# Value projections of a head moved one step later, their turns between and behind the block-inverse products

## What is computed

```python
q = silu(conv4(LN(x) @ Wq))                    # 8 heads of 128
k, v = silu(conv4(LN(x) @ Wk)), silu(conv4(LN(x) @ Wv))   # two keys and two values per token
q, k = q / |q| / sqrt(128), k / |k|
beta, g = 2 * sigmoid(LN(x) @ Wb), -exp(A_log) * softplus(LN(x) @ Wa + dt_bias)
for t in range(256):                           # per head, state 128 x 128
    state *= exp(g[t])
    for j in range(2):
        state += outer(k[t, j], (v[t, j] - k[t, j] @ state) * beta[t, j])
    o[t] = q[t] @ state
x += (rms(o) * norm_w * silu(LN(x) @ Wg)) @ Wo
x += top-k-masked, symmetrised similarity of ctx (256 x 256 per sequence) mixed with LN(x)
x += shared expert + two routed experts of eight, on LN(x)
```

## Time and profile before

| | us |
|---|---|
| median of 3 runs | 935.14 (933.33 to 941.7) |
| the profiled execution | 941.6, span 939.8 |
| attention part of its span (steps 0 to 10) | about 634 |
| busy: PE / DVE / ACT / POOL | 841.2 / 519.8 / 422.1 / 344.9 |

### The profile page before, as it was taken

One profiled execution on the slowest core, in us unless ns is written; L12 is line 12 of the kernel. 1 busy time (PEld: TensorE's weight loads), 2 busy tenths in 40 slices (PEclk: granted clock), 3 DMA queues, 4 the chain that ended last, 5 costly groups with the idle time before them and its releaser, 6 DMA issues. The chain is left out here.

```text
span 939.8 us, 16187 instructions
## 1 busy us (share of the span) xinstructions
PE 841.2 (90%) x5500; PEld 610.6 (65%) x5501; DVE 519.8 (55%) x1259; ACT 422.1 (45%) x929; POOL 344.9 (37%) x654
## 2 busy tenths in 40 slices
PE   4767999899999999999999876975999999999992
PEld 3333486686786776866867765864667667676761
DVE  3664638778887897887888655466411111111113
ACT  2656757456655656656666234213222222222220
POOL 1127466357368456564673480003420000000015
PEclk9879969879989899799899777796999999999997
DMA  7504133123150141141201301009673100110104
GB/s 187 141 25 111 23 85 90 24 59 67 24 121 5 38 109 21 31 98 24 56 19 24 89 2 29 2 1 366 238 241 109 33 24 32 33 33 22 33 24 128
DMA packets 107362, 66.30 MB, mean 71 GB/s; under 512 B 64864, under 2 KB 98720, under 8 KB 107296
## 3 DMA queue, kind: packets, MB, share of 16 engines
q1 hardware_dynamic: 99904, 59.52, 24.0%
q0 software_dynamic: 1536, 4.20, 1.5%
q10 hardware_dynamic: 5856, 1.73, 0.8%
HBM read 50.84 MB, written 14.58 MB: 70 GB/s over the span
## 5 line engine op out<-in xcount | busy, mean ns | idle before, releaser
L1129 DVE SCALAR_TENSOR_TENSOR y<-bank,cwh,y 128x510 f32<-128x510 f32 (+2 forms) x240 | 177.1, 743 | 57.9 <-ACT y L883 53.7
L633 PE MATMUL bank<-xnT,wbuf 128*128 128x512 f32 x320 | 163.0, 635 | 7.3 <-DVE y L1129 7.3
L1668 PE MATMUL bank<-f_wgu,f_xgT 128*128 x368 | 118.8, 466 | 0.0
L1946 DVE TENSOR_TENSOR f_act<-f_sg,bank 128x352 f32<-128x352 f32 x62 | 32.2, 521 | 143.8 <-PE bank L1668 141.5
L1433 POOL TENSOR_TENSOR term<-inv,blk 128x126 f32<-128x126 f32 (+22 forms) x248 | 87.8, 354 | 57.9 <-DMA blk<-a_blocks 39.1
L1785 ACT ACTIVATE f_sg<-bank 128x352 f32<-128x352 f32 x62 | 28.7, 464 | 161.1 <-PE bank L1668 152.7
L633 PEld LDWEIGHTS bank<-xnT,wbuf 128*128 128x128 f32 x320 | 57.9, 199 | 66.4 <-issue 53.8
L2021 POOL DMA_INDIRECT f_back<-slots_y,f_slot x16 | 15.4, 963 | 231.5 <-DMA slots_y<-f_yb 224.9
L1436 POOL TENSOR_TENSOR inv<-inv,term 128x126 f32<-128x126 f32 (+22 forms) x248 | 91.5, 369 | 19.4
L1713 PE MATMUL bank<-f_wdn,f_actT 128*128 (+1 forms) x372 | 91.5, 388 | 1.0 <-ACT f_actT L1798 0.8
L1668 PEld LDWEIGHTS bank<-f_wgu,f_xgT 128*128 128x128 f32 x368 | 66.2, 190 | 36.8 <-issue 7.6
(11 more groups left out here) (209 smaller groups left out, 1537.4 us busy)
## 6 DMA issues: line engine op xcount, KB each, us to landing
f_wgu<-in_exp_gu SPq DMA_DIRECT2D x8, 1408.0 KB, 9.7
f_wdn<-in_exp_dn SPq DMA_DIRECT2D x8, 640.0 KB, 10.5
dr<-sums SPq DMA_DIRECT2D x16, 256.0 KB, 4.5
ex<-sums SPq DMA_DIRECT2D x16, 256.0 KB, 4.5
blk<-a_blocks SPq DMA_DIRECT2D x16, 256.0 KB, 4.0
slots_x<-oT SPq DMA_DIRECT2D x24, 128.0 KB, 1.9
f_xg<-slots_x SPq DMA_DIRECT2D x24, 128.0 KB, 2.0
slots_y<-f_yb SPq DMA_DIRECT2D x23, 128.0 KB, 1.7
```

The source lines that it names most:

```text
L633: last = mm(bankA[p % 2][:, :], wbuf[A.par][:, kt, wblk, :], xnT[:, kt, (p % 2) * 512:(p % 2 + 1) * 512], start=kt == 0, stop=kt == 1)
L1129: v.scalar_tensor_tensor(out=y[p % 2][:, :, k:], in0=src[:, :, 0:SEQ - k], scalar=cwh[A.par][:, cb, 3 - k:4 - k], in1=y[p % 2][:, :, k:], ...
L1668: last = mm(gu[c][:, 0:FFH], xt[:, k, :], wgu[:, e, k, at:at + FFH], start=k == 0, stop=k == 1)
L1946: v.tensor_tensor(av[:, par, half * FFH:(half + 1) * FFH], sg[:, half, :], gu[2 * half + 1][:, 0:FFH], ALU.mult).then_inc(f_act, 1)
```

## The change

**Projections.** `projection(slot, A, B)` gives slots 0 to 5 to the keys and queries of head s and slots 6 to 9 to the values of head s-1. Step 0 thus has six projections, step 8 has four (before: ten and none), steps 1 to 7 have ten. All counts on `proj_done`, `conv_step` and `silu_done` follow `nth`. The value weights have a semaphore and a wait of their own.

**Turns.** The four `vtok` items move from slots 1, 2, 3 and 5 to slot 11 (behind t32), "blocks of 64" (behind x32) and LAST (behind p64, and behind t64). The two gates go to slots 3 and 5.

**Ends.** In step 0 `scalar_values` comes a slot earlier and without its exponentials; these, `dm` and `ex` stand in slot 11 (step 1: slot 8). The sixth norm stands in slot 11. 20 of the 24 zeroing DMAs go to step 1. `gwT` is loaded behind step 1's scatter. In step 8 top-k is spread: 8, then 4 operations in slots 1 to 3, 2 of the next tile in slots 4 to 8, and 10 at the end; `sigmoids` go to slot 9. The tap copies (`taps`) stand at POOL's end. The waits inside POOL's `norm`, and the order `dx`, `kn`, `sh`, `qE`, are untouched.

```diff
+        3: {"B": [("gate", 0)]},
+        5: {"B": [("gate", 1)]},
...
+        11: {"B": [("t32", 0), ("t32", 1), ("vtok", 0)]},
+        BLOCKS_64: {"B": [("x32", 0), ("x32", 1), ("vtok", 1)]},
+        LAST: {"B": [("p64", 0), ("p64", 1), ("vtok", 2), ("t64", 0), ("t64", 1), ("vtok", 3)]}}
...
-SCALARS_AT = 3
-EXP_AT = {0: 7, 1: 2}
+SCALARS_AT = 2
+EXP_AT = {0: 11, 1: 8}
+
+def projection(slot, A, B):
+    X = A if slot < 6 else B
+    return (X, slot) if X else None
...
-            for i in range(5):
+            for i in range(3):
                 sp.dma_start(wbuf[h % 2][:, :, i, :], head_weights(i, h)).then_inc(w_in[h % 2], 16)
+        def value_weights(h):
+            if h >= 2:
+                sp.wait_ge(proj_done, nth(h - 2, 9))
...
-        for m in range(SLOT_TILES):
-            sp.dma_start(dram["slots_x"][m], zero).then_inc(slots_zeroed, 16)
+        zero_slots(0, 4)
...
-                if b == 0 and kind != "kend":
-                    pe.wait_ge(silu_done, 10 * h + {"pair": 6, "vtok": 10}[kind])
+                if b == 0 and kind == "pair":
+                    pe.wait_ge(silu_done, nth(h, 5))
+                if b % 2 == 0 and kind == "vtok":
+                    pe.wait_ge(silu_done, nth(h, 8 + b // 2))
...
-                if A and slot < 10:
-                    proj(A, slot)
+                if slot < 10 and projection(slot, A, B):
+                    proj(*projection(slot, A, B))
...
-                if not A and tiles and slot == 5:
-                    topk(tiles[0], 8, 2 * ROUNDS)
+                if not A and tiles and 1 <= slot <= 3:
+                    topk(tiles[0], 4 * slot + 4, 4 * slot + 8)
+                if not A and tiles and 4 <= slot <= 8:
+                    topk(tiles[1], 2 * slot - 8, 2 * slot - 6)
...
-            if A:
-                start(A)
             if A and A.h == 0:
+                taps(0)
+                taps(1)
```

More of the change, by code:

```diff
@@ L105 @@
 FILL = {FIRST: {"B": [("pair", n) for n in range(BC // 2)]},
[L106 to L110, removed]
+        1: {"E": [("out", 0)]},
+        3: {"B": [("gate", 0)]},
+        4: {"E": [("out", 1)]},
+        5: {"B": [("gate", 1)]},
         6: {"B": [("kend", 0)]},
@@ L121, with projection_table, nth @@
 B_BANKS = 3
-SCALARS_AT = 3
-EXP_AT = {0: 7, 1: 2}
+SCALARS_AT = 2
[3 more added lines that the diff above has]
+    return (X, slot) if X else None
+def projection_table():
+    out = []
+    run_heads(lambda A, B, C, E: out.extend(projection(slot, A, B) for slot in range(10)))
+    return {(x[0].h, x[1]): i for i, x in enumerate(x for x in out if x)}
+PROJECTION = projection_table()
+def nth(h, p):
+    return PROJECTION[h, p] + 1
 def items_at(place):
@@ L361, in attention @@
     w_in = [w_in0, w_in1]
+    wv_in = [sem(f"wv_in{i}") for i in range(2)]
     wo_in = [wo_in0, wo_in1]
@@ L443, in sync_program, with zero_slots @@
         sp.wait_ge(zero_done, 1)
-        for m in range(SLOT_TILES):
-            sp.dma_start(dram["slots_x"][m], zero).then_inc(slots_zeroed, 16)
-        for k in range(KT_H):
-            sp.dma_start(gwT[:, k, :], dram["gate_w"].rearrange("e (k p) -> k p e", p=P)[k], allow_slow_non_contiguous=True).then_inc(mix_in, 16)
+        def zero_slots(first, end):
+            for m in range(first, end):
+                sp.dma_start(dram["slots_x"][m], zero).then_inc(slots_zeroed, 16)
+        zero_slots(0, 4)
         blocks = a_blocks.rearrange("(p x) -> p x", x=NB * NB)
@@ L502, in step @@
                 loads(A.h + 1)
+            if A and A.h:
+                value_weights(A.h)
             if 2 <= s <= HEADS:
@@ L530, in step @@
                 difference_rows(A.h + 1)
+            if s == 1:
+                zero_slots(4, SLOT_TILES)
             if B:
@@ L535, in step @@
             if s == 1:
+                for k in range(KT_H):
+                    sp.dma_start(gwT[:, k, :], dram["gate_w"].rearrange("e (k p) -> k p e", p=P)[k], allow_slow_non_contiguous=True).then_inc(mix_in, 16)
                 tiles_out()
@@ L1041, in step @@
             if A and s not in EXP_AT:
+                exp_table()
                 decays(A)
@@ L1055, in step @@
                     scalar_values()
-                if slot == EXP_AT.get(s, -1):
-                    decays(A)
-                    pair_decays(A)
                 if s == 1 and slot < 11:
                     context_copies(act, slot, slot + 1)
-                if s == HEADS and slot == 7:
+                if 2 <= slot and projection(slot - 2, A, B):
+                    silu(*projection(slot - 2, A, B))
+                if s == HEADS and slot == 9:
                     sigmoids()
-                if A and 2 <= slot:
-                    silu(A, slot - 2)
                 if A and 5 <= slot <= 10:
                     square(A, slot - 5)
-                if A and slot < 10:
-                    evac(A, slot)
+                if slot < 10 and projection(slot, A, B):
+                    evac(*projection(slot, A, B))
+                if slot == EXP_AT.get(s, -1):
+                    exp_table()
+                    pair_decays(A)
+                    decays(A)
+                    if s == 0:
+                        scalar_decays()
             fill(BLOCKS_64)
@@ L1299, in step @@
                     gate_ends()
-                if A and 1 <= slot <= 10:
-                    conv(A, slot - 1, (1,))
+                todo = projection(slot - 1, A, B) if 1 <= slot <= 10 else None
+                if todo:
+                    conv(*todo, (1,))
                 if C:
                     scan(C, slot)
-                if A and 1 <= slot <= 10:
-                    conv(A, slot - 1, (2, 3))
+                if todo:
+                    conv(*todo, (2, 3))
                 fill(slot)
@@ L1328, in step @@
                     norm_sum(A, 1)
+            if not A and tiles:
+                topk(tiles[1], 10, 2 * ROUNDS)
             fill(LAST)
@@ L1340, in gpsimd_program, with taps @@
         pool.wait_ge(small_in, 160)
-        def start(A):
-            h = A.h
-            if not isinstance(h, int) or h >= 2:
-                if some(30 * (h - 1)):
-                    pool.wait_ge(conv_step, 30 * (h - 1))
-            g.tensor_copy(cwh[A.par][:, :, :].rearrange("p a k -> p (a k)"),
+        def taps(h):
+            if h >= 2:
+                pool.wait_ge(conv_step, 3 * nth(h - 2, 9))
+            g.tensor_copy(cwh[h % 2][:, :, :].rearrange("p a k -> p (a k)"),
                           cw[:, :, :, :].rearrange("p h a k -> p h (a k)")[:, h, :]).then_inc(cwh_done, 1)
```

76 lines of the change are left out of this document (42 added, 34 removed).

## The result

The changed kernel takes 979.6 us (978.32 to 982.69, 4 runs) against 936.29 us of the kernel before (933.33 to 941.7, 4 runs): 1.046 times as long, 95% interval 1.040 to 1.052. The forecast was 986, slower by over 1% with a chance of 0.85. The sum came out near; several of its terms did not.

What follows compares the result with a forecast made beforehand. The prediction took PE's own work and the loop through POOL's inversion as level bounds. Terms -18 + 3.2 + 14.4 + 5 x (7.4 + 3.2) - 1.6 = +51 us, on the 935.1 median, gave 986 us, range 950 to 1010.

Steps and rivals of the forecast that it cites:

- The wait of `kn`: POOL's `kn` waits about 7 us for late `vtok`; `qE` ends at T+7.0 (T: start of a step's pair products).
- From `ex` to the inversion: Late `ex` and `keep_k` delay ACT's gathering DMAs; POOL's inversion starts at T+22.8 instead of T+15.4, +7.4 us per full step.
- The two delays lie beside one another: PE, standing some 6 us in slots 1 and 2, reaches p32 about T+57; the inverted blocks come at T+58.2.
- The tail: From p32 to the next pair products, four value turns add +3.2 us per step, bounds +1.8 to +6.5.
- Step 1: Inversion starts as before, only the tail is longer: +3.2 us; moved zeroing DMAs cost 0, at most 3.
- Step 2: SP gathers late behind `ex`, `gwT` and similarity stores: inversion at T+26.9 instead of T+15.7, +11.2 us, plus +3.2 tail.
- Step 0 and step 8: Step 0 loses four projections and waits, -18 us; step 8's spread top-k lets p32 follow the blocks, -1.6 with its tail.
- The sum: Whole kernel: the steps' terms add to +51 us, giving 986 us, +5.4%.
- Part absorbed: Rival: slack in the inversion loop hides part of the delay, +3 instead of +7.4 per step: 960 us, chance 0.15.
- Faster: Rival: the `kn` wait costs nothing since late `ex` does not hold ACT's DMAs: 923 us, chance 0.10.
- cancelled: Rival: step 0's gain and the losses cancel, about 3 us per full step: 935 us, chance 0.05.
- Lower clock: Rival: the wait in slots 1 and 2 and the turns hold PE's clock down, tails +6.5: 1005 us, chance 0.15.

Runs made afterwards that it cites:

- gather_first: The changed kernel with ACT's two gathering DMAs ahead of `ex` in ACT's step, `kn` still waiting for `vtok`: 980.57 us.
- v_back: The changed kernel with projections, value turns and gates back in their earlier slots, the rest of the change kept: 926.38 us.
- two_kn: The changed kernel with a second `kn` buffer, so `kn` waits only for the `vtok` copies of two heads ago: 975.96 us.
- two_kn_mm: two_kn with the value turns and the tail's x32 turns as ordinary products with the identity instead of transpose mode: 990.76 us.
- exp_early: The changed kernel with `dm` and `ex` of step 1 in slot 2 instead of slot 8: 970.65 us.
- stores_first: The changed kernel with `gwT`, the four similarity stores and the first tile's load ahead of `ex` in SP's step 1: 971.54 us.
- v_back_ordered: v_back with step 1's `dm` and `ex` in slot 2 and similarity stores ahead of `ex` in SP's step 1: 917.34 us.
- combo: The changed kernel with the edits of two_kn, exp_early and stores_first together: 957.07 us.
- combo_gate: combo with the second gate product moved from slot 5 into LAST, ahead of the third turn of values: 965.13 us.
- turns_last: The changed kernel, one `kn`, with the four value turns in one piece behind the last t64 products: 996.86 us.
- two_kn_last: two_kn with the four value turns and their copies in one piece behind the last t64 products: 954.51 us.

## Why the forecast was right, and where its steps were not

**The wait of `kn`.** Right in every sign it promised: 8.31 us put down to `vtok` (about 7 promised), `qE` ended at T+7.2 (7.0), `ex` on ACT at T+12.1 (12.0).

**From `ex` to the inversion: mis-sized.** The step "The exponential and `keep_k` take 3.14: T+15.1" failed. ACT's DMAs were issued 0.20 us behind the *start* of `ex`, not behind the end of `keep_k`; in the earlier trace rows they had stood 3.14 us behind it because they waited for `aT`. So the inversion begins at T+18.9 to T+19.8 instead of T+22.8, +3.9 and not +7.4. I had also blamed ACT's queue alone; gather_first shows that SP's six, behind `ex` and `qE`, bind nearly as late.

**"The two delays lie beside one another"** was right, but the larger is the one I called smaller. PE's front (6.70 us) puts p32 at T+56.5 to T+57.6 (forecast 57 for PE, 58.2 for the blocks): +6.4 where I had +7.4. That the term came out near is partly luck: its size was worked out for the inversion, which moved by half of it.

**The tail: mis-sized.** "+3.2 us per tail" failed for steps 3 to 7: +0.2. Two things cancelled. At a clock of 1.00 the tail is 14.07 us with the turns; the shortest without them was 12.53 us at 0.93 (step 6; v_back has the same in step 3), so they add at least 1.5 us. And the low stretch that the tail had before (14.14 us at 0.78) has moved to T+14. The upper bound of +6.5 was too low as well: I took 17.0 us from step 2, whose tail lacks the output product of stage E, and where full steps did run their tails low (two_kn) they took 22.4, +8.2 against 14.2. The rule of the Trainium skill (TensorE: Matmul & The Clock Gate, Part 4: PE-mode transpose), that a transpose "doesn't count as PE-busy the same way", would have put these tails at their upper end. They ran at a clock of 1.00 with 16 more turns in them, so here it did not come out as I had read it; whether it has a part in the low tails of two_kn stays open, since two_kn_mm changed the work too.

**Step 1: the largest miss.** "All other edits ... I cost them at 0, the zeroing at up to 3 us" failed. `dm` in slot 8 holds `dr`, `dr` the zeroing, the zeroing (9.93 us) the inverses; exp_early gives the price, 10.5 us of step 1. The zeroing alone was harmless (exp_early has it, and p32 at T+50.6); a late `dm` without it was not run. I had looked at the queue of the moved DMAs but not at what its head waited for. The tail adds 5.1 at the low clock (0.50 throughout).

**Step 2** came as worked out: +10.6 up to p32 (11.2), +3.3 in the tail. stores_first takes 7.4 us of it back.

**Step 0 and step 8** were near: -18.2 (-18), -3.2 (-1.6; p32 at T+48.3, the tail 22 us). v_back reaches its first T at 53.8, v_back_ordered at 49.2, the kernels with moved projections at 40.8 to 45.9. So 3 to 13 us of step 0's gain belong to the moved projections; the split is rough.

**The sum** was +51, the spans differ by 41: 12 too little in step 1, 20 too much in steps 3 to 7. The time was foretold better than its parts, and that is luck: the two errors have nothing to do with one another. Of the small readings, the inversion takes 27.2 us and not 27.3, and began at T+15.5 on average and not T+15.4; neither changes the sum.

**Rivals.** *Part absorbed* (960) had its size of +3 close to what the inversion did, but the front took its place. *Faster* (923) and *cancelled* fell. *Lower clock* did not happen in full steps of the changed kernel (step 5 at 0.93 against 0.92; over the whole program 0.900 against 0.905), though steps 1 and 2 fell to 0.75 and 0.79, from 0.84 and 0.85. It is what happens once the wait is gone: two_kn. The premise I had not questioned was that the cost of a wait comes back when the wait is removed. Here the wait of 6.7 us and a low tail of 8.3 us more are alternatives, and the change costs about 6.6 us per full step by either. Which of them one calls the cause depends on which is removed first; to get back to 64.7 both must go, as in v_back, or in steps 6 and 7 of combo (64.1 and 64.4 us), which hold the moved values and turns, with `kn` free and little or no low stretch.

**Open.** What makes the clock fall in the tail. The transpose mode alone does not account for it (two_kn_mm); whether thin work does, combo_gate could not tell. What the profiles show is where the clock fell: 1 to 2 us behind the start of p32 in two_kn, 8 to 11 us behind it in the kernel before, inside PE's wait in the changed kernel. combo shows that the same code can pass the tail at either level.

## What to carry to other kernels

When items are moved to the end of a step, list what is queued behind every single-buffered tile that they read, on each queue in turn; and when a producer is moved on one engine, follow the DMA that waits for it and everything issued behind that DMA. A wait taken off PE is a gain only if the granted clock holds: read the clock of the stretch behind it, and compare the length of identical work at both levels. A change made of many parts is best undone by parts: here the small edits at the ends gained some 6 us, and the large one lost 53.

## What the runs showed that I had not expected

ACT sends DMAs while its own earlier activation is still running: issue at 363.19, `ex` from 362.99 to 364.05.

The place of the same four turns is worth +17 us with one `kn` (turns_last) and -21 us with two (two_kn_last). In the one tail of turns_last that ran wholly at full clock it was worth 0.6 us; the other tails differ in how much of them ran at the low level.

Identical instructions from p32 to T took 14.05 us at a clock of 1.00 and 22.87 at 0.51 in one execution, and combo, whose tails pass at either level, varies by 3% from one execution to the next (935.51 to 964.52), while the changed kernel with its wait varies by 0.4%.
